# A transformer's norms in more slots: modulation after the transpose, the inverse root on GpSimd

## The reference, cut to what matters

```python
for l in (0, 1, 2):                                  # the three blocks
    mod = silu(c) @ w_mod + b_mod                    # 6 vectors of 144 for each batch
    sh_msa, sc_msa, g_msa, sh_mlp, sc_mlp, g_mlp = split(mod, 6)
    h = (x - mean) * rsqrt(var + 1e-6) * (1 + sc_msa) + sh_msa
    q, k, v = h @ w_qkv + b_qkv                      # 16 heads of 9; l == 1: q, k normed with gains
    o = softmax(q @ k.T * 9 ** -0.5) @ v
    x = x + g_msa * (o @ w_proj + b_proj)
    h = (x - mean) * rsqrt(var + 1e-6) * (1 + sc_mlp) + sh_mlp
    x = x + g_mlp * mlp(h)                           # l == 0: four experts, the best two by a gate
U = qr(P).Q                                          # P is 144x64
R = expm(A)                                          # A 64x64 skew, from silu(c) @ W.T + b
return x + (x @ U @ R - x @ U) @ U.T
```

## Time and profile before

| | |
|---|---|
| median of 3 runs | 911.35 us (909.35 to 921.39) |
| the profiled execution | 919.2 us, its span 917.2 us |
| mean granted clock of PE in it | 0.856 |
| busy, share of the span | PE 751.5 us (82%), DVE 556.0 (61%), ACT 386.0 (42%), POOL 181.0 (20%) |

### The profile page before, as it was taken

How to read it: one execution, slowest core, us unless ns; L and a number is a source line. 1 busy time by engine, 2 the same in 40 slices (tenths; PEclk the granted TensorE clock), 3 DMA queues, 4 the chain that set the end, 5 groups by cost and what they waited for, 6 DMA issues and landing times.

```text
span 917.2 us, 11092 instructions
## 1 busy us (share of the span) xinstructions
PE 751.5 (82%) x3571; PEld 438.5 (48%) x3571; DVE 556.0 (61%) x1614; ACT 386.0 (42%) x690; POOL 181.0 (20%) x372
## 2 busy tenths in 40 slices
PE   6597889967998799798867886979897789979746
PEld 1353444335764445366444343645443555436325
DVE  3477787886327558752465777474787666785242
ACT  0221465534444544254235442435453356646511
POOL 5502012440132300302323003021003110021020
PEclk9955899989997669799977997976897988999957
DMA  3210100110121000012100000100000101000000
GB/s 88 69 35 7 32 14 22 39 31 13 48 56 32 1 24 13 12 33 60 39 18 1 24 12 13 32 1 1 24 13 11 33 1 25 12 12 1 13 1 13
DMA packets 22714, 21.23 MB, mean 23 GB/s; under 512 B 4831, under 2 KB 17015, under 8 KB 22658
## 3 DMA queue, kind: packets, MB, share of 16 engines
q1 hardware_dynamic: 22610, 20.52, 8.6%
q10 hardware_dynamic: 48, 0.02, 0.0%
HBM read 13.62 MB, written 0.61 MB: 16 GB/s over the span
## 4 chain that ended last, share of the span: by engine, by line
PE 62%; DVE 28%; issue 4%; ACT 2%; POOL 2%; DMA 0%; DVEq 0%; SPq 0%; ACTq 0%; POOLq 0%
PE m_bank L1400 11%; PE o_bank L1422 10%; DVE row_max L972 9%; PE s_bank L1383 8%; PE d_bank L1539 7%; PE d_bank L1483 3%; PE m_bank L1592 3%; PE m_bank L1409 2%; DVE h_tok L1031 2%; PE d_bank L1528 2%; PE d_bank L1440 2%; PE d_bank L1439 1%; PE d_bank L1454 1%; PE d_bank L1530 1%; PE d_bank L1529 1%
## 5 line engine op out<-in xcount | busy, mean ns | idle before, releaser
L797 ACT ACTIVATE probs<-s_bank 128x512 f32<-128x512 f32 x384 | 223.1, 598 | 380.4 <-PE s_bank L1383 377.1
L972 DVE TENSOR_REDUCE row_max<-m_bank 128x1 fp32r<-128x512 f32 x384 | 255.3, 686 | 91.8 <-PE m_bank L1400 86.5
L1400 PE MATMUL m_bank<-k_pad,q_t 128*128 128x512 f32 x348 | 173.1, 511 | 43.0 <-DVE row_max L972 12.6
L1383 PE MATMUL s_bank<-q_t,k_pad 128*128 128x512 f32 x384 | 176.3, 466 | 2.9 <-ACT probs L797 2.0
L1400 PEld LDWEIGHTS m_bank<-k_pad,q_t 128*128 128x128 f32 x348 | 72.1, 212 | 115.0 <-issue 36.8
L1422 PE MATMUL o_bank<-probs,v_aug 128*32 128x512 f32 x768 | 120.6, 704 | 0.7 <-ACT probs L797 0.7
L1383 PEld LDWEIGHTS s_bank<-q_t,k_pad 128*128 128x128 f32 x384 | 81.8, 215 | 30.1 <-ACT probs L797 15.4
L1539 PE MATMUL d_bank<-w,g_act 128*128 128x144 f32 (+1 forms) x480 | 61.8, 288 | 8.7 <-issue 8.7
L1539 PEld LDWEIGHTS d_bank<-w,g_act 128*128 128x128 f32 (+1 forms) x480 | 59.5, 190 | 14.2 <-issue 8.3
L714 POOL TENSOR_TENSOR h_tok<-h_tok,mod 128x144 f32<-128x144 f32 x48 | 23.7, 494 | 202.7 <-DVE h_tok L1031 202.7
L1592 PE MATMUL m_bank<-gram_rows,ident 64*64 64x208 f32 (+42 forms) x128 | 40.3, 403 | 16.0 <-DVE gram_rows L1207 15.6
(11 more groups left out here) (232 smaller groups left out, 1145.1 us busy)
## 6 DMA issues: line engine op xcount, KB each, us to landing
k_pad<-k_t SPq DMA_DIRECT2D x96, 64.0 KB, 2.0
raw_a<-in_L_cond_w_dram SPq DMA_DIRECT2D x10, 288.0 KB
w<-in_L_cond_w_dram SPq DMA_DIRECT2D x10, 288.0 KB
w_rows<-in_L_cond_W_dram SPq DMA_DIRECT2D x8, 141.8 KB
raw_d<-in_L_cond_w_dram SPq DMA_DIRECT2D x30, 36.0 KB
x_tok<-in_x_dram SPq DMA_DIRECT2D x2, 288.0 KB, 4.5
w<-in_L_cond_W_fc_dram SPq DMA_DIRECT2D x2, 288.0 KB
raw_a<-in_L_cond_W_fc_dram SPq DMA_DIRECT2D x2, 288.0 KB
```

The source lines that it names most:

```text
L797: act.activation(probs[:, n % PROBS, :], s_banks[n % S_BANKS][:, :], ACT.Exp, scale=HD ** -0.5)\
L972: dve.tensor_reduce(row_max[:, grp % 2, t, MAXROW + 32 * j:MAXROW + 32 * j + 1], bk[:, :], AX.X, ALU.max).then_inc(drained, 1)
L1383: pe.matmul(s_banks[n % S_BANKS][:, :], k_pad[:, grp % PADS, j, kt * P:(kt + 1) * P], q_t[:, par, g, :], start=True, stop=True).then_inc(s ...
L1400: ins = pe.matmul(bk[:, :], q_t[:, par, g, t * P:(t + 1) * P], k_pad[:, grp % PADS, j, :], start=True, stop=True)
```

## The change: what it does

**Slots.** "msa" and "mlp" norms get five slots in place of three: (1) DVE's statistics, (2) the inverse root, (3) DVE's normalisation and Pool's copy of the rest channels, (4, 5) the transposes and the passes behind them. "o" and "x" become a stage "lay" of three slots, whose tiles PE transposes directly from `o_tok` and `x_tok`, which are widened to the layout of `h_tok`.

**The inverse root** is computed by Pool in slot 2, in 14 instructions on 128x4 that depend on one another (L730 to L736): add epsilon, a first value from the bits, three Newton steps. DVE waits in slot 3 for the semaphore `rooted`.

**Modulation** moves behind the transpose, where channels are partitions: ACT writes `h_hi` and `h_d` with a scale and a shift for each partition; DVE computes the same in float32 (`h_part` for the middle rows of the rest, `h_full` for the 128), then `h_lo` = `h_full` - `h_hi`; Pool does the subtraction for the middle of `h_d`. Pool's two instructions per tile go.

**Vectors.** "mods" now computes four vectors as columns, for both batches at once, with 32 small matmuls (two columns each) into one bank; "gates" computes the two gate vectors across partitions as before. Both are issued once a layer: mods of layer 1 and 2 in blocks 1 and 3, gates of the layers in blocks 0, 2 and 4. In block 0 "gates" takes the place of "mods" 1 in the list, and now stands ahead of prep 1; the weights of layer 1 ("ada" 1) are no longer loaded in the head but sorted by `load_order`, behind the last slot of "gates" 0, and those of layer 2 behind "gates" 1.

```diff
     if block == 0:
-        out += [("norm", 1, "msa"), ("qkv", 1), ("prep", 1), ("prep", 2), ("mods", 1, 0), ("prep", 3)]
+        out += [("norm", 1, "msa"), ("qkv", 1), ("gates", 0), ("prep", 1), ("prep", 2), ("prep", 3)]
...
     if block == 1:
-        out += [("mods", 1, 1)]
+        out += [("mods", 1)]
     if block == 2:
-        out += [("mods", 2, 0), ("prep", LAYER_ITEM[2])]
+        out += [("gates", 1), ("prep", LAYER_ITEM[2])]
     if block == 3:
-        out += [("mods", 2, 1)]
+        out += [("mods", 2)]
     if 1 <= block < BLOCKS - 1:
         out += [("norm", block + 1, "msa"), ("qkv", block + 1)]
+    if block == BLOCKS - 2:
+        out += [("gates", 2)]
     if block == BLOCKS - 1:
...
 def after_attention(block):
-    out = [("norm", block, "o"), ("proj", block), ("norm", block, "mlp")]
+    out = [("lay", block, "o"), ("proj", block), ("norm", block, "mlp")]
     if block // B == 0:
...
-HEAD = [("mods", 0, 0), ("mods", 0, 1), ("prep", 0), ("norm", 0, "msa"), ("qkv", 0)]
-TAIL = after_attention(BLOCKS - 1) + [("norm", BLOCKS - 1, "x"), ("rotate", 1)]
+HEAD = [("mods", 0), ("prep", 0), ("norm", 0, "msa"), ("qkv", 0)]
+TAIL = after_attention(BLOCKS - 1) + [("lay", BLOCKS - 1, "x"), ("rotate", 1)]
...
-BANKS_OF = {"prep": (), "mods": (2,), "norm": (0, 2, 0), "qkv": (2, 2, 0, 2, 2, 2, 2), "proj": (2,), "gate": (1, 0),
+BANKS_OF = {"prep": (), "mods": (1,), "gates": (2,), "norm": (0, 0, 0, 2, 0), "lay": (0, 2, 0), "qkv": (2, 2, 0, 2, 2, 2, 2), "proj": (2,), "gate": (1, 0),
             "mlp": (7, 0), "rotate": (2,)}
...
-ROOM = {"prep": (), "mods": (1,), "norm": (4, 1, 2), "qkv": (2, 2, 1, 2, 2, 2, 2), "proj": (2,), "gate": (2, 1),
+ROOM = {"prep": (), "mods": (1,), "gates": (1,), "norm": (2, 1, 2, 1, 2), "lay": (2, 1, 2), "qkv": (2, 2, 1, 2, 2, 2, 2), "proj": (2,), "gate": (2, 1),
         "mlp": (1, 1), "rotate": (1,)}
...
-HEAD_FROM = 3
+HEAD_FROM = 4
...
-    todo += [(LAST_SLOT[("mods", 1, 1)], ("ada", 2))]
+    todo += [(LAST_SLOT[("gates", l - 1)], ("ada", l)) for l in range(1, LAYERS)]
...
-                    sp.wait_ge(s["mods_part"], 4 * l)
+                    sp.wait_ge(s["mods_full"], 3 * l)
...
-            load_ada(1)
...
             def norm(blk, kind):
...
+                if kind in ("msa", "mlp"):
+                    yield
+                    n = seen.next("rooted")
+                    pool.wait_ge(s["aggregated"], T * n)
+                    y, v, r = rstd[:, :], var_eps[:, :], nwt[:, 0, :]
+                    link(pool.tensor_scalar(v, mean_var[:, :, 1], EPS, None, ALU.add))
+                    link(pool.tensor_scalar(y.bitcast(I32), v.bitcast(I32), -0.5, 1597463007.0, ALU.mult, ALU.add))
+                    for i in range(3):
+                        link(pool.tensor_tensor(r, v, y, ALU.mult))
+                        link(pool.tensor_tensor(r, r, y, ALU.mult))
+                        link(pool.tensor_scalar(r, r, -0.5, 1.5, ALU.mult, ALU.add))
+                        ins = pool.tensor_tensor(y, y, r, ALU.mult)
+                        if i < 2:
+                            link(ins)
+                    ins.then_inc(s["rooted"], 1)
+                    pool.wait_ge(s["rooted"], n)
+                    yield
                 if kind == "o":
                     pool.wait_ge(s["o_taken"], G * (blk + 1))
...
+                for t in range(T):
+                    if kind == "x":
+                        pool.wait_ge(s["x_done"], blk % B * 2 + t // 2 + 1)
+                    elif kind != "o":
+                        pool.wait_ge(s["xn_ready"], seen.next("xn_ready"))
+                    tile = token_tile(blk, kind, t)
+                    pool.tensor_copy(tile[:, P + 32:P + DW].rearrange("p (r w) -> p r w", r=2)[:, :, 0:CR],
+                                     tile[:, P:C].unsqueeze(1).to_broadcast([P, 2, CR]))\
+                        .then_inc(s["h_tok_ready"], 1)
+                    pool.wait_ge(s["h_tok_ready"], seen.next("h_tok_ready"))
+                yield
+                _, (_, d_free, before) = ring.take(), ring.take()
+                yield
                 seen.next("norm")
...
+                if kind in ("msa", "mlp"):
+                    pool.wait_ge(s["h_part_ready"], seen.next("modulated"))
+                    pool.wait_ge(s["h_d_ready"], seen.n["norm"])
+                    pool.tensor_tensor(h_d[32:64, :], h_part[32:64, :], h_d[32:64, :].bitcast(F32), ALU.subtract)\
...
+                act.wait_ge(*mods_done[l])
+                act.wait_ge(s["mods_ready"], 3 * (l + 1))
+                shift, scale = mod_a[:, l % 2, v, b:b + 1], mod_a[:, l % 2, v + 1, b:b + 1]
+                act.activation(h_hi[:, :], a_bank[:, :], ACT.Identity, scale=scale, bias=shift)\
+                    .then_inc(s["h_hi_ready"], 1)
+                act.wait_ge(s["h_part_ready"], seen.next("modulated"))
+                act.activation(h_d[:, :], d_bank[0:DW, :], ACT.Identity, scale=mod_d[:, l % 2, v + 1, b:b + 1],
+                               bias=mod_d[:, l % 2, v, b:b + 1]).then_inc(s["h_d_ready"], 1)
                 yield
...
+                    for i in range(T):
+                        dve.bn_stats(stat[:, i, :], x_tok[:, b, i, 0:C]).then_inc(s["dve_done"], 1)
+                    done[0] += T
+                    fill[0]()
+                    dve.wait_ge(s["dve_done"], done[0])
+                    for i in range(T):
+                        dve.bn_aggr(mean_var[:, i, :], stat[:, i, :]).then_inc(s["aggregated"], 1)
+                    n = seen.next("rooted")
+                    yield
+                    yield
+                    fill[0]()
+                    dve.wait_ge(s["aggregated"], T * n)
+                    dve.wait_ge(s["rooted"], n)
                     if seen.n.get("norm", 0):
                         dve.wait_ge(s["h_turned"], T * seen.n["norm"])
                     else:
                         dve.wait_ge(s["consts_ready"], 1)
                     for t in range(T):
...
+                        dve.tensor_scalar(h_tok[:, t, 0:C], x_tok[:, b, t, 0:C], mean_var[:, t, 0:1], rstd[:, t:t + 1],
+                                          ALU.subtract, ALU.mult).then_inc(s["xn_ready"], 1)
                 seen.next("norm")
                 yield
                 (a_bank, a_free, _), (d_bank, d_free, _) = ring.take(), ring.take()
                 yield
                 fill[0]()
...
+                else:
+                    dve.wait_ge(s["h_turned"], T * seen.n["norm"])
+                    dve.tensor_scalar(h_part[32:64, :], d_bank[32:64, :], mod_d[32:64, l % 2, v + 1, b:b + 1],
+                                      mod_d[32:64, l % 2, v, b:b + 1], ALU.mult, ALU.add)\
+                        .then_inc(s["h_part_ready"], 1)
+                    dve.wait_ge(s["h_hi_ready"], seen.n["norm"])
+                    link(dve.tensor_scalar(h_full[:, :], a_bank[:, :], mod_a[:, l % 2, v + 1, b:b + 1],
+                                           mod_a[:, l % 2, v, b:b + 1], ALU.mult, ALU.add))
+                    dve.tensor_tensor(h_lo[:, :], h_full[:, :], h_hi[:, :].bitcast(F32), ALU.subtract)\
+                        .then_inc(a_free, 1)
                 yield
...
+            def mods(l):
+                bk, _ = take(ring)
+                pe.wait_ge(ada_in, 48 * (l + 1))
+                pe.wait_ge(s["c_wide"], 2)
+                for i, v in enumerate((0, 1, 3, 4)):
+                    for ada, c, first in ((ada_a, c_wide_a, True), (ada_d, c_wide_d, False)):
+                        pe.matmul(bk[:, B * i:B * (i + 1)], ada[:, v * C:v * C + P], c[:, :, 0], start=first,
+                                  stop=not first)
+                    for ada, c, first in ((ada_a, c_wide_a, True), (ada_d, c_wide_d, False)):
+                        for r in range(0, DW, 32):
+                            ins = pe.matmul(bk[r:r + 32, B * (4 + i):B * (5 + i)], ada[:, v * C + P:v * C + P + 32],
+                                            c[:, :, 0], start=first, stop=not first, skip_group_check=True)
+                ins.then_inc(s["mods_full"], 1)
+                yield
+
...
-                    pe.transpose(d_bank[0:DW, cols], h_tok[:, t, P:P + DW], ident[:, :]).then_inc(s["h_turned"], 1)
+                    pe.wait_ge(s["h_tok_ready"], seen.next("h_tok_ready"))
+                    cols, tile = slice(t * P, (t + 1) * P), token_tile(blk, kind, t)
+                    pe.transpose(a_bank[:, cols], tile[:, 0:P], ident[:, :])
+                    pe.transpose(d_bank[0:DW, cols], tile[:, P:P + DW], ident[:, :]).then_inc(s["h_turned"], 1)
```

204 lines of the change are left out of this document (110 added, 94 removed).

## The result

The changed kernel takes 948.21 us (median of 4 runs, 946.02 to 951.48), the kernel before 914.28 (4 runs, 909.35 to 921.39): the ratio is 1.0368, with a 95% interval of 1.0284 to 1.0452. It is slower by 34 us. The forecast was 910, with a range up to 932. The profiled execution took 946.72 us.

A forecast was written before the change was run, and what follows sets the result against it. Neither PE (82% busy) nor DVE (61%) was taken as full; they hand each other work. Terms −28 −10 +2.5 +28 +2 +4 = −1.5 us, put on the median of 911.35, gave 910, range 886 to 932.

The forecast's parts named there:

- SP's queue, +28 and +2: Block 1's first o_tok turn: items 2 and 3 load later, delaying the program 28 us (25 to 31); low clock adds 2.
- Rival (4): The SP queue stall does not appear, since the data come sooner than read: 882 us; chance 0.05.
- The norms, -28: Eight norm windows gain 26 us, the middle of 19 and 34, from less DVE work; block 0's first norm adds 2.
- "+0.9": Head: h_d now goes DVE, ACT, Pool, with Pool's subtraction some 1.25 us where DVE took 0.68; adds 0.9 us.
- The 75% and 92%: Busy shares of DVE (75%) and PE (92%) in attention without a norm, used to price the gain in the norm windows.
- Rival (1): The norms give all they can: DVE at 95% in the eight windows, −46 us there, 885 in all; chance 0.22.
- The root on Pool: Each norm's Pool root takes 3.8 us; DVE would stand 1 to 2 us in two-step norms, little in the rest.
- Rival (2): Slower: DVE waits for Pool's root in its third slot, PE stands as before; norms −4, 936 us; chance 0.13.
- Head and tail, -10: Head gains 6 us (mods, modulation, less root); tail gains 1.5 and 2.5; together −10, bounds −15 and −4.
- Mods and gates, +2.5: PE in the body: two mods and three gates, 14 to 22 us, replace four old mods of 15 us; +2.5.
- Block 3's norm, +4: Norm in block 3's slot (block 2): item 11 loads behind ada 2, Pool's root queues behind it; +4 us (0 to +7).
- Rival (3), the shared port: DVE instructions with two SBUF inputs, such as h_lo, are blocked by Pool's h_d subtraction: +10 us, 920; chance 0.10.

The follow-up runs named there:

- f1: The changed kernel with items 2 and 3 back in their exact old place in the DMA order, behind pads 4 and 5, ahead of the second skew rows; ratio 1.0051.
- f4: The kernel before with only its msa and mlp norms put in five slots, root still on DVE, modulation and DMA order untouched; ratio 1.0058.
- h1: f2 with the first and last norms' root on DVE, and PE waiting for h_d only before a linear layer's fourth product; ratio 0.9760.
- h2: g3 with the root of the first and last norm on DVE and PE's late wait for h_d, old modulation; ratio 0.9736.
- g2: f2 with the inverse root computed by DVE instead of Pool in slot 2 of all twelve norms; ratio 1.0050.
- f2: f1 with the modulation weights of layer 2 loaded behind item 11 in place of in front of it; ratio 0.9931.
- h3: g3 with DVE also running the eleven root instructions in the second slot, into scratch that nothing reads; ratio 1.0026.
- g3: f4 with the root on Pool in slot 2 in place of DVE, modulation stays old; ratio 0.9909.
- e1: The changed kernel with items 2 and 3 sorted early again, which put them in front of pads 4 and 5; ratio 1.0193.
- e3: e1 with the modulation weights of layer 2 sorted behind item 11 in place of in front of it; ratio 1.0068.
- g5: The kernel before with six Newton steps in place of three for the root of each norm; ratio 1.0183.

## Why the prediction was wrong, by its steps

**SP's queue, +28 and +2.** Right, and the largest term: PE stood 26.48 us where 25 to 31 were given, and with the items in place 29 us went. Item 2 was issued at 180.06 in place of 160.40, in a program that was 4.6 us ahead here (the scores of step 64 at 173.23, before at 177.86): 24.3 us later, where 25 to 26.5 had been said. Rival (4) is refuted.

**The norms, -28: the step that failed.** f1, the changed kernel with this stall alone removed, stands at +0.5% where the other terms had promised -3.4%. What is left for the norms, when the other terms are taken at what they measured below, lies between 2 us won and 6 lost (an estimate: 4.7 us of the ratio, plus 5.6 to 8.7 won in head and tail, less 1.3 of mods and gates and 6.4 to 11 of block 3's norm; the interval of f1 adds 6 us either way), in place of 28 won.

I had said that PE's idle time would shrink because DVE's work in the windows shrinks, by the shares at which DVE and PE run in undisturbed attention. DVE's work did shrink, by 23 us over all, and so did the waits that the earlier trace rows shows: in f1 by 31.8 us in front of the `m_bank`s. But PE is in order, and there are two more places where it waits for a norm. In f1 it stands 19.2 us more in front of the first products and 13.7 more in front of the turns, and so nothing is left. Four of its lines:

```profile
L1492 PE MATMUL m_bank<-k_pad,q_t 128*128 128x512 f32 x348 | 170.8, 502 | 23.3 <-DVE lu L1335 10.4 <-DVE row_max L1037 7.5 <-DVE gram_rows L1299 3.8
...
L1637 PE MATMUL d_bank<-h_hi,ff_hi 128*128 128x512 f32 (+1 forms) x60 | 28.2, 470 | 17.4 <-POOL h_d L762 10.1 <-ACT g_act L941 3.7 <-DVE moe L1225 2.5
...
L1456 PE MATMUL d_bank<-lay_hi,h_hi 128*128 128x432 f32 (+2 forms) x56 | 20.7, 370 | 14.9 <-POOL h_d L762 7.8 <-DVE h_d L1122 7.1
...
L1563 PE MATMUL d_bank<-ident,h_tok 128*128 128x128 f32 x48 | 16.9, 365 | 27.7 <-POOL h_tok L751 27.6
```

f4, the split with nothing of the new modulation, shows the same move: 29.7 us less in front of the `m_bank`s, 16.8 more in front of the turns, 5.9 more in front of the first products. I priced neither the wait in front of the turns nor the new chain behind them (0.80 + 0.78 + 1.70 us where 0.6 + 0.68 had been; "+0.9" stood in the terms of head and tail, and not in that of the norms between them). h1 takes 11.1 us of the wait in front of the first products away, and 1.0 to 1.3% of time with it; but h2 shows that the old form had such a gain to give too, so it isn't all a price of the new chain. The 75% and 92% were shares and no chain, and it is on shares that the term rested. Rival (1) made more of the same shares and is refuted too.

**The root on Pool.** The 3.8 us were right (3.9 in all twelve norms, instructions 0.28 us apart), and so was a wait of 1 to 2 us in single norms (one of 3.0 lay above it). But DVE stood for it in eight norms, 25.0 us in all, by its line:

```profile
L1109 DVE TENSOR_SCALAR h_tok<-x_tok,mean_var,rstd 128x144 f32<-128x144 f32 x48 | 13.8, 351 | 25.0 <-POOL rstd L736 13.1 <-issue 11.9
```

8.9 us of them are head and tail, 8.0 the norm behind item 11, 3.0, 2.1, 1.3, 1.1 and 0.6 five others. Rival (2) came nearest in the size, with norms of -4, but not in the cause: g2 has no such wait, its idle time is 6.0 us lower, and it is no faster. The Trainium skill, GPSIMD Engine Reference, § 3.1 Elementwise, keeps "use DVE for elementwise" as the rule. This chain took 3.9 us on Pool and 2.2 on DVE, and it was still better on Pool by 1.2% (f2 against g2; h3 against g3 shows what the eleven instructions cost DVE); in head and tail DVE's root made the gaps shorter. Here the measurement decides.

**Head and tail, -10.** The 32 small matmuls took 5.9 us (9.60 to 15.45) where I had taken 9, the first normalisation stands at 22.36, and the first qkv product at 30.47, 5.1 us earlier than the earlier trace rows (I had said 6):

```profile
9.60 0.56 PE L1530 MATMUL d_bank<-c_wide_a,ada_a 128*128 128x2 f32 x2 [9.60 <-DVE c_wide_d L1030]
...
16.20 0.94 DVE L1092 BATCH_NORM_STATS2 stat<-x_tok 128x6 f32<-128x144 f32 x4
...
22.36 1.15 DVE L1109 TENSOR_SCALAR h_tok<-x_tok,mean_var,rstd 128x144 f32<-128x144 f32 x4 [4.80 <-issue]
...
30.47 0.70 PE L1455 MATMUL d_bank<-lay_hi,h_hi 128*128 128x432 f32 x1 [2.90 <-POOL h_d L761]
```

By the first scores only 2.0 us of it were left (71.55 against 73.58): PE's small products in between were at the low level here (0.91 us for the pair L1700 at 39.74) and at the high level before (0.53 for L1592 at 43.08). This differs from one execution to the next, for e1, e3, f1 and f2 have the same head as the changed kernel. The same pair in f1, then in f2:

```profile
37.87 0.53 PE L1701 MATMUL m_bank<-gram_rows,ident 64*64 64x205 f32 x2 [1.12 <-DVE gram_rows L1299]
```

```profile
39.68 0.91 PE L1701 MATMUL m_bank<-gram_rows,ident 64*64 64x205 f32 x2 [1.12 <-DVE gram_rows L1299]
```

In f1 and e3 the pair was at the high level and the first scores stand at 68.5, 5.1 us earlier than before; in f2 and e1 it was at the low level and they stand at 71.5. So the head kept 2 to 5 us, by luck of the clock. The mean granted clock of 0.863, over 0.856 as I had said it would be, is no sign of a faster PE: the windows view gives 1.00 for the first 40 us of the changed kernel, though a pair of the same line took 0.95 us in them, at 37.68. The tail, from the last scores to the end, is 3.6 us shorter (47.5 against 51.1), as said.

**Mods and gates, +2.5.** With the head's part taken off, and overlaps counted once, they took 15.9 us of PE in place of 14.6: about even.

**Block 3's norm, +4.** Right in kind: Pool's preparation from 491.93, the root from 496.25, DVE idle for 8.04 us where 9 had been said. The gap of 7.87 is followed by another of 3.77; moving `ada` 2 made the first one 3.16 us and left the second, and gave 6.4 us of idle time back over all.

**Rival (3), the shared port.** Seen and small: single DVE instructions with two inputs in SBUF stretch beside Pool's subtraction, in five of twelve norms by 0.5 to 0.8 us, 3.2 us in all. Three of the five are of this line (ns min, median, max):

```profile
L1333 DVE TENSOR_TENSOR s_small<-lu,s_small x64: 151/151/666, 395.9 to 790.6; 64x1 f32<-64x1 f32 x64
```

That a DVE instruction with two inputs in SBUF stretches beside a Pool instruction that reads SBUF agrees with the Trainium skill, SBUF — State Buffer, § Who interferes with whom. Its 3.2 us are a third of the +10 that the rival gave it. On the other side `h_tok` became faster, 351 ns in place of 468, since Pool no longer modulates beside it: with the old modulation it took 469 and 472 in f4 and g3.

## What to carry to other kernels

Where a table of steps also sorts a DMA queue, compare the queue before and after an edit that only moves compute: here one key was worth 25 us in the one kernel and 29 in the other. When work is taken off an engine that others wait for, follow PE's next wait behind it before counting the gain, since an engine that goes in order waits at the next place; then put each wait in front of the first instruction that reads the data, not in front of the stage. A share of busy time is no price for a gap. A run that lengthens the gap by a known amount (g5) gives one for more of the same, but not for taking gaps away (f4).

## What was not expected

The root's eleven small instructions on DVE cost 1.2 to 1.5%, though PE's idle time is lower with them (g2 against f2, f4 against g3), or higher by less than the time (h3 against g3, 7.9 us). And PE's busy time for the same matmuls went from 757.2 to 740.8 us between two kernels that differ in the place of one load: at this size a single span says little.
